# Five start-up loads of a fused decoder layer change places in the sync engine's queue

## What is computed

```python
x = x + attn(layernorm(x), Wq, Wk, Wv, Wp)                 # causal, 16 heads of 32, 4 key heads, rotary
x = x + xattn(layernorm(x), ctx, Wq, w_kc_q, w_kc_kv, W_qr, W_kr, Wo)
x = x + moe(layernorm(x), gate, bias, w1, w2, w3, shared)  # 8 experts, top 2, and a shared one
# inside xattn, for 16 heads h:
kv_rope = kv_c * cos + rotate_half(kv_c) * sin
q_r = einsum("bshq,hqr->bhsr", einsum("bshk,hkq->bshq", x @ Wq.T, w_kc_q), W_qr)
k_r = einsum("bld,hdr->bhlr", kv_rope, W_kr)
ctx_c = softmax(q_r @ k_r.T) @ kv_rope
out = (ctx_c through w_kc_kv) @ Wo.T
```

## Time and profile before

| | |
|---|---|
| median of three runs | 574.41 us (574.02 to 574.89) |
| span of the profiled execution | 573.5 us |
| TensorE busy | 545.9 us, 95% of the span |
| VectorE, ScalarE, GpSimd busy | 67%, 52%, 54% |
| granted TensorE clock, mean | 0.991 |
| DMA in the first eight of 40 slices (115 us) | 8 9 7 7 6 5 4 7 tenths busy |

### The profile page before, as it was taken

One profiled execution on the slowest core, in us unless ns is written; L12 is line 12 of the kernel. 1 busy time (PEld: TensorE's weight loads), 2 busy tenths in 40 slices (PEclk: granted clock), 3 DMA queues, 4 the chain that ended last, 5 costly groups with the idle time before them and its releaser, 6 DMA issues. The chain is left out here.

```text
span 573.5 us, 9651 instructions
## 1 busy us (share of the span) xinstructions
PE 545.9 (95%) x3446; PEld 431.1 (75%) x3449; DVE 383.3 (67%) x872; ACT 296.2 (52%) x668; POOL 307.5 (54%) x358
## 2 busy tenths in 40 slices
PE   5989999999989999999999999999999999999886
PEld 4666766766667889878898888888898988886343
DVE  5786897895874776457565566674676647686763
ACT  3235634436564766447765367663577643522340
POOL 0689654556715568405975048862178534662560
PEclk9999999999999999999999999999999999799998
DMA  8977654777551502215894337034150037217527
GB/s 263 261 264 243 219 160 144 264 223 215 211 179 55 181 1 38 37 47 157 260 257 110 101 119 190 13 74 74 41 217 1 2 114 327 68 61 150 146 83 265
DMA packets 47009, 83.64 MB, mean 146 GB/s; under 512 B 20018, under 2 KB 28036, under 8 KB 46068
## 3 DMA queue, kind: packets, MB, share of 16 engines
q1 hardware_dynamic: 43716, 70.47, 38.6%
q0 software_dynamic: 2224, 10.73, 8.3%
q10 hardware_dynamic: 1024, 1.84, 0.9%
HBM read 63.09 MB, written 29.77 MB: 162 GB/s over the span
## 5 line engine op out<-in xcount | busy, mean ns | idle before, releaser
L1883 POOL TENSOR_TENSOR xprob<-xprob,erec 128x375 f32<-128x375 f32 x112 | 91.4, 826 | 125.3 <-DVE erec L1560 124.7
L1203 ACT ACTIVATE xprob<-s_ps,nmax 128x375 f32<-128x375 f32 x112 | 64.3, 575 | 54.6 <-DVE nmax L1555 52.1
L1555 DVE TENSOR_REDUCE nmax<-s_ps 128x1 f32<-128x375 f32 x112 | 59.6, 538 | 0.2 <-PE s_ps L63 0.2
L61 PE MATMUL k_ps<-ow,ctx_hl 128*112 128x512 f32 x128 | 52.4, 410 | 0.3 <-DVE ctx_hl L1550 0.3
L1530 DVE TENSOR_TENSOR pt_hl<-f_ps,pt_hl 125x384 fp32r<-125x384 f32 (+1 forms) x62 | 38.2, 616 | 21.5 <-ACT pt_hl L1175 20.6
L63 PE MATMUL k_ps<-ow,ctx_hl 128*112 128x512 f32 x128 | 50.5, 394 | 0.0
L62 PE MATMUL k_ps<-ow,ctx_hl 128*112 128x512 f32 x128 | 50.3, 393 | 0.0
L1550 DVE TENSOR_TENSOR ctx_hl<-k_ps,ctx_hl 128x448 fp32r<-128x448 f32 x32 | 20.0, 625 | 42.5 <-ACT ctx_hl L1198 42.5
L1876 POOL TENSOR_TENSOR prob<-prob,rec 112x1792 f32<-112x1792 f32 x8 | 25.5, 3185 | 39.6 <-DVE rec L1496 39.4
L61 PE MATMUL s_ps<-kvt,qt_hl 128*128 128x376 f32 x112 | 44.5, 397 | 0.7 <-ACT xprob L1203 0.4
L1894 POOL TENSOR_TENSOR ow<-ow_raw,ow 128x1024 fp32r<-128x1024 f32 x16 | 38.3, 2396 | 7.2 <-ACT ow L1213 7.1
(11 more groups left out here) (354 smaller groups left out, 1520.5 us busy)
## 6 DMA issues: line engine op xcount, KB each, us to landing
ow_raw<-ow_dram SPq DMA_DIRECT2D x16, 512.0 KB, 3.5
w<-w_dram SPq DMA_DIRECT2D x6, 1024.0 KB, 10.0
raw_b<-in_raw SPq DMA_DIRECT2D x8, 640.0 KB, 4.9
raw_m<-in_raw SPq DMA_DIRECT2D x8, 576.0 KB, 6.8
raw_q<-in_raw SPq DMA_DIRECT2D x8, 512.0 KB, 7.4
ow_dram<-bw_sb SPq DMA_DIRECT2D x8, 512.0 KB, 5.6
qw_raw<-aw_dram SPq DMA_DIRECT2D x16, 256.0 KB, 3.5
w_dram<-in_w POOLq DMA_DIRECT2D x8, 512.0 KB, 5.5
```

The lines of the kernel that those rows point to most:

```text
L61: pe.matmul(out, a_hl[0], b_hl[0], start=start, stop=False, skip_group_check=True)
L1203: act.activation(xprob[z][:, 0:L], s_bank(n, k)[:, 0:L], ACT.Exp, bias=nmax[:, z:z + 1], accum_out=esum[:, z:z + 1]).then_inc(xexp_done, 1)
L1555: dve.tensor_reduce(nmax[:, z:z + 1], s_bank(n, k)[:, 0:L], X, ALU.max, negate=True).then_inc(xmax_done, 1)
L1883: pool.tensor_tensor(xprob[z][:, 0:L], xprob[z][:, 0:L], erec[:, z:z + 1].broadcast_to([128, L]), ALU.mult).then_inc(xp_ready, 1)
```

## The change

In SP's list `load_b(0)` moves from behind the context to ahead of the tables kcos and ksin, and `load_q(0)` from behind `load_b(0)` to ahead of the first context. The tables and the context so stand one and two places of weights further back. Nothing else changes.

```diff
             load_x(1)
             sp.dma_start(mask[:, :, :], a["mask"]).then_inc(mask_loaded, 16)
             load_m(0)
+            load_b(0)
             sp.dma_start(kcos[:, :, :], a["kcos"]).then_inc(rope_tab, 16)
             sp.dma_start(ksin[:, :, :], a["ksin"]).then_inc(rope_tab, 16)
+            load_q(0)
             load_ctx(0)
-            load_b(0)
-            load_q(0)
             for j in range(2, ROUNDS):
                 load_x(j)
```

## The result

The changed kernel takes 576.61 us (median of 20 runs, 574.21 to 578.64) against 572.62 us for the kernel before in the same comparison (median of 20 runs, 569.11 to 574.89). The ratio is 1.0071, 95% interval 1.0055 to 1.0087: slower by 0.7%, or 4.0 us. The three times of before that the prediction started from lie at the upper end of these twenty.

The account below looks back on a forecast made before the run. TensorE, busy 95% of the span, was taken to bound the kernel. Terms 2.3 - 0.3 - 0.25 - 0.3 gave +1.45, say +1.5 us, on a median of 574.41: 575.9 us, range 574.0 to 576.8.

Parts of the forecast that it names:

- the rival in which nothing is swallowed: Start-up delay: lane takes its upper bound (+2.9) or both ACT waits move too; 576.4 to 577.1 us, chance 0.12.
- Nothing to gain from the early weights: TensorE's first uses of raw_b and raw_q: it did not wait for them, so moving them forward gives 0.
- When the context lands: First context's load: lands at 24.9 us after the change, 21.2 before; POOL's rotation starts 2.3 us later than 22.60.
- slow lane: Start-up loads: 125-row tables pile up on the same five DMA engines, 2.15 us each, holding up loads behind them.
- the last of them ends when the last of them ended before: Five reordered start-up loads: the context, now last, lands at raw_q's old 24.90 us.
- One for one into TensorE: POOL's first rotation to TensorE's turning of rk: a later rotation delays TensorE equally, 28.50 to 30.8, +2.3 us.
- second store wait: ACT's 0.31 us wait at 57.95 and TensorE's 0.32 us idle at 63.94 close: -0.3 us, bounds 0 and -0.3.
- DVE's slack: DVE's row maximum at 31.89, 0.3 us after TensorE's scores end: this slack absorbs delay, -0.3 us.
- ACT's wait at 43.6: ACT's wait for kvt_hl's store still ends near 43.6; TensorE's 0.45 us wait for at_sb shrinks to 0.2: -0.25 us.
- What is late at 64 us stays late: After 64 us nothing waits for a landing until the routed experts, so everything stays 1.5 us later.

Follow-up runs that it names:

- version with fillers: Changed kernel plus unused filler matmuls in TensorE's three idle stretches before its first scores (15, 4 and 3), against the kernel before: 578.99 us, ratio 1.0032.
- split tables: Changed kernel with every load of kcos, ksin and a context issued as two, of 112 and 13 rows, against the kernel before: 572.31 us, ratio 0.9999.
- context last behind the tables: Kernel before with raw_b and raw_q both moved ahead of the first context but behind tables kcos and ksin: 577.00 us, ratio 1.0077.
- nine fillers: Changed kernel plus nine unused filler matmuls of 448 columns ahead of turning the first context, against the kernel before: 577.25 us, ratio 1.0071.
- four tables: Kernel before with the second context's load moved up behind the first's, so four 125-row loads precede raw_b: 571.92 us in one run.

## Why the prediction was right, and where it was wrong

The direction, the place and the mechanism of the late context were right; the fall of the clock was missing. 576.61 us lies inside the range, but by luck. The size was not right: +1.5 us forecast, +4.0 measured, more than the 2.0 to 2.9 us of the rival in which nothing is swallowed. By the prediction's own steps:

- **Nothing to gain from the early weights.** Right in the profile at hand: TensorE waits for raw_b neither before nor after. On a second chip the kernel before did wait 0.55 us for raw_b; the change itself was not timed on that chip, only its version with fillers (1.0032).
- **When the context lands.** The mechanism (a slow lane of transfers of 125 rows) is shown by the split tables. The size was off: 24.9 forecast, 26.37 measured. The landings of the changed kernel give the terms: raw_b 17.24 - 14.78 = 2.46 us and not 2.05; kcos, ksin and raw_q together 23.87 - 17.24 = 6.63, and the context 26.37 - 23.87 = 2.50 and not 2.15. If kcos and ksin took 2.50 each as well, raw_q's share is 1.63, as put. So most of the 1.47 us is in the three transfers of 125 rows; the second profile of the kernel before also has them at 7.27 / 3 = 2.42 each. The step that failed is "the last of them ends when the last of them ended before". From raw_m's landing to that of the last of the five it takes 10.1 and 10.6 us in the two profiles of the kernel before and 10.8 with raw_b alone moved, but 11.6, 11.5, 11.2 and 11.1 in the four profiles with the changed kernel's order (two of them with fillers), 11.0 with the context last behind the tables, and 11.3 with raw_q alone moved, where raw_b is last. Why the same loads need more time in some orders was not found.
- **One for one into TensorE.** Right to 0.24 us: POOL 3.77 later, rk's turning 3.53. POOL's work in between was that much shorter, most of it the addition of rq (1.27 us and not 1.45); why was not looked into.
- **The clock.** Missing altogether. The prediction moved durations and assumed that they keep their length. Idle time of 3.83 us cost another 1.3 us at 1.2 GHz, which is the difference between +3.53 at rk and +4.84 at the end of the scores (35.20 + 1.23 against 30.54 + 1.05), and which the fillers took away. It comes on top of the error of the landing, 1.5 us; the second store wait, which swallowed more than forecast (below), hid 0.6 us of the two.
- **DVE's slack.** 0.3 forecast, 0.20 measured (+4.84 to +4.64).
- **ACT's wait at 43.6.** Right but for 0.4 us: 43.62 before, 43.98 after, so the store landed that little later, and TensorE's wait for at_sb shrank from 0.45 to 0.21; the delay fell by 0.23, forecast as 0.25.
- **The second store wait.** Forecast 0.3, with 0.3 as its upper bound; ACT indeed no longer waits. TensorE's turning of prob at 62.21 comes at 66.62, still 4.41 later, its scores at 64.86 come at 68.34, 3.48 later: 0.9 us went there, with its waits for kvt_hl and aw_sb.
- **What is late at 64 us stays late.** Right: +3.5 at 65 and at 215 us, +3.4 at 488.

The sum as measured: 3.77 - 0.24 + 1.31 - 0.20 - 0.23 - 0.9 = 3.5 us, against 4.0 in the medians. The range held because its base, 574.41, was itself 1.8 us above the median of the larger set, which made up for most of the missing 2.5 us. From 572.62 the same steps give 574.1 us and the same range 572.2 to 575.0, and 576.61 lies outside it. It even lies where the prediction put the rival in which nothing is swallowed (576.4 to 577.1); yet later waits swallowed 1.4 us (from +4.84 to +3.48).

## What to carry to other kernels

Before a load is moved up, ask who waits for it, and then who waits for every load that it is moved past; here the first list was empty in the first profile, and the second had one name on it. Transfers of 125 rows (187.5 KB) delayed what was queued behind them by 1.9 to 2.5 us each here, and the same bytes in pieces of 112 and 13 rows did not: try such a split before reordering anything around a transfer of this kind. Other numbers of rows were not tried. And where an edit adds idle time to TensorE, price the time at half clock that may follow, not the idle time alone.

## What the runs showed of the hardware that was not expected

- The order of the same five loads changed their total by about a microsecond: 10.1 and 10.6 us from raw_m's landing in the order of before, 10.8 to 11.6 in the four other orders. The last load's form does not decide it: with raw_b last it is 11.3.
- Idle time of 2.5 us in three pieces, the last ending 3.6 us after the first began (nine fillers), still let the granted clock fall; 1.74 us (raw_b alone moved) did not, nor did a single wait of 1.51 us (four tables).
- The routed experts at the end took 3 us more in one of the two profiles than in the other, which hid the whole effect from a comparison of two profiled spans.
- Landings at the start differ by 1.6 us between the two profiles of the kernel before (raw_b at 23.26 and at 7.27 + 17.6 = 24.87), more than the margins on which its order of loads rests.
